# Scores of two heads side by side on 64 rows each, and a new order of work for a pair of heads

## The chip, the cores and the metric

The kernel runs on one core of one Trainium2 chip. The metric is the time on the device of one execution, in microseconds; three runs of the kernel before took 1910.01, 1911.17 and 1916.82 us, and their median is 1911.17 us.

## The reference

A gated cross-attention layer is followed by a gated mixture of experts, all in float32. The input x has 8 batches of 512 tokens of 256 features, the context 8 batches of 1024 keys.

```
q = layernorm(x) @ Wq; k = ctx @ Wk; v = ctx @ Wv        # 8 heads of 64
attn = softmax(q k^T / 8) v, per head
x = x + tanh(g0) * (attn @ Wo + bo)
h = layernorm(x); probs = softmax(h @ router^T)           # 8 experts, the top 2 of each token
pre, gate = rows @ W1[e]^T, rows @ Wg[e]^T                # rows: the tokens of expert e, up to 1280
x = x + tanh(g1) * sum over the two experts of weight * ((pre * silu(gate)) @ W2[e]^T)
```

## The kernel before

Each float32 operand of a product is split into a high part (rounded to the type fp32r, in which TensorE takes one pass) and a low part (the rest); a product is then three matmuls: high by high, high by low and low by high (`passes`, L776 to L781). ScalarE makes the high parts (`hi`), VectorE the low ones (`lo`, L1205).

The attention works batch by batch. A batch is a body of 32 steps; START, FIRST and LAST are written out, six middle batches run in a loop, END finishes the last one. A unit is one head and 128 query tokens (32 units a batch): 128x1024 scores. Unit n = u goes through the engines in steps: TensorE makes its scores in step u (`make_scores`), VectorE their negated maximum (L1491), ScalarE the exponents with the row sum (L1120, a step later), VectorE the reciprocal of the sum (L1501), GpSimd scales the row (L678), TensorE transposes it in eight 128x128 pieces (`turn`, in step u + 2), ScalarE and VectorE split the transposed halves into pt_h and pt_l (in step u + 3). The scores are in four PSUM banks, two units; the transposed unit is in two banks, and `turn` waits until VectorE has read the half that it overwrites (L812).

In the scores the 128 rows of the array hold one head twice: k_st has the 64 rows of a head's high part of k, and in the other 64 rows its low part, q_h has the high part of q twice, and q_l its low part twice. Four matmuls of 512 columns then make one unit (L798 to L804).

The other two PSUM banks are a ring. Everything else that TensorE computes is a job that fills the next bank of the ring: q, k and v projections of the heads to come, o (attention output of one head and 256 tokens, sixteen matmuls), w (its product with Wo for 128 tokens), x and h (transposes of the normalised input of the next batch and of the normalised sum of the batch before), l (router logits) and r (ranks of the tokens in the experts' lists). The table `JOBS` (L70) says in which step a job is done; o jobs stand in the odd steps (L98). ScalarE and VectorE empty the banks of step u - 1 in step u (`drain`, L1043 and L1364): its first job ahead of the other work of the step, its second after the maximum. A job waits until the bank two jobs back is empty (L928). A q result is written to both halves of the rows by four instructions on 64 partitions on each of the two engines, a k result by two.

`between` (L1433) puts the steps of layer normalisation and routing, small VectorE instructions that each wait for the one before, in five gaps of a step. GpSimd also normalises (L655), splits the next batch's context (`split_ctx`), adds the bias (L704, once a batch in step 15) and issues the scatter of the routed rows (L666).

The wait of the score matmuls and the order of TensorE in a step are:

```
until(pe, exp_done, at(b, UNITS, u - 1))      # the unit two before is exponentiated
...
make_scores(body, u); the jobs of step u; turn(body, u - 2)
```

After the last batch the kernel ranks tokens and pads lists, and then runs the experts: 36 chunks of 256 rows, three split matmuls per product, TensorE without a break.

## Time and profile before

| | |
|---|---|
| median of three runs | 1911.17 us |
| the profiled execution, and its span | 1914.74 us, 1913.0 us |
| TensorE busy (L801 scores: 512 + 512 matmuls) | 1749.2 us, 91% of the span |
| VectorE, ScalarE, GpSimd busy | 1396.8, 1124.2, 686.6 us |
| mean granted clock of TensorE | 0.973 of full |

Busy time is the union of the instructions of an engine. The ends of matmuls are modelled and overlap the next ones, so what a matmul occupies is read from the starts of two blocks in the time line, not from its printed length.

### The profile page before, as it was taken

To read this page: it belongs to the slowest core of one execution; us is meant where nothing else is said; L and a number is where in the kernel's file an instruction comes from. 1 tells how busy PE (TensorE), PEld (TensorE's weight loads), DVE (VectorE), ACT (ScalarE), POOL (GpSimd) and SP (SyncE) were. 2 spreads that over 40 slices of the span, in tenths; PEclk is the share of its full clock that TensorE was granted. 3 is DMA by queue.
4 is the path that set the end of the run, shared out by engine and by line. 5 is a ranking of instruction groups with operands and counts; after the bars stand their busy time and mean duration, and the time that the engine had idled before them with its cause. 6 is when DMAs were issued, how large, how long until landed. Compare 5 with 4: busy or idle time off the path is not lost. (4 is left out here: it accounts for less than half of the span.)

```text
span 1913.0 us, 38524 instructions
## 1 busy us (share of the span) xinstructions
PE 1749.2 (91%) x12942; PEld 1629.6 (85%) x12943; DVE 1396.8 (73%) x2955; ACT 1124.2 (59%) x2259; POOL 686.6 (36%) x619
## 2 busy tenths in 40 slices
PE   5899998998998998998998999559999999999998
PEld 4788887987887887887887888459999999999998
DVE  5888888888898888889898888655545645555443
ACT  4767656666766666666776776334545545445443
POOL 3352344344244245244343433423332322333232
PEclk9999999999999999999999999779999999999999
DMA  6100001001011001000000002233133132231211
GB/s 180 34 12 12 23 24 35 23 23 35 12 34 35 12 23 40 18 23 31 16 23 28 18 23 76 91 104 98 30 100 94 28 99 62 61 98 28 33 28 28
DMA packets 65148, 85.88 MB, mean 45 GB/s; under 512 B 7208, under 2 KB 53800, under 8 KB 65008
## 3 DMA queue, kind: packets, MB, share of 16 engines
q1 hardware_dynamic: 47680, 64.08, 10.6%
q0 software_dynamic: 15984, 18.82, 5.6%
q8 instruction: 78, 1.28, 0.3%
q10 hardware_dynamic: 1344, 1.20, 0.2%
q14 instruction: 62, 0.51, 0.1%
HBM read 54.59 MB, written 29.48 MB: 44 GB/s over the span
## 5 line engine op out<-in xcount | busy, mean ns | idle before, releaser
L678 POOL TENSOR_SCALAR probs<-probs,row_rec 128x1024 f32<-128x1024 f32 x256 | 287.7, 1124 | 704.4 <-DVE row_rec L1501 673.9
L1036 ACT ACTIVATE pt_h<-turned 128x512 fp32r<-128x512 f32 x512 | 279.8, 597 | 199.1 <-PE turned L814 194.7
L1207 DVE TENSOR_TENSOR pt_l<-turned,pt_h 128x512 fp32r<-128x512 f32 x512 | 333.6, 684 | 78.4 <-ACT pt_h L1036 76.2
L1491 DVE TENSOR_REDUCE neg_max<-scores 128x1 f32<-128x1024 f32 x256 | 310.9, 1214 | 2.0 <-PE scores L801 1.9
L1120 ACT ACTIVATE probs<-scores,neg_max 128x1024 f32<-128x1024 f32 x256 | 287.2, 1122 | 3.4 <-DVE neg_max L1491 2.4
L814 PE MATMUL turned<-ident,probs 128*128 128x128 f32 x2048 | 272.6, 277 | 10.8 <-POOL probs L678 6.0
L915 PE MATMUL ring<-pt_h,v_hl 128*128 128x256 f32 x1024 | 254.0, 286 | 24.3 <-DVE q_l L1404 9.2
L1658 DVE TENSOR_TENSOR act_f<-ffn,silu 128x256 f32<-128x256 f32 x288 | 122.1, 424 | 193.1 <-ACT silu L1161 180.1
L814 PEld LDWEIGHTS turned<-ident,probs 128*128 128x128 f32 x2048 | 235.3, 143 | 23.5 <-POOL probs L678 10.2
L915 PE MATMUL ring<-pt_l,v_hl 128*128 128x256 f32 x1024 | 251.4, 284 | 0.0
L1161 ACT ACTIVATE silu<-ffn 128x256 f32<-128x256 f32 x288 | 110.4, 383 | 220.3 <-PE ffn L781 212.4
L915 PEld LDWEIGHTS ring<-pt_h,v_hl 128*128 128x128 f32 x1024 | 195.9, 191 | 41.9 <-issue 32.6
L760 POOL DMA_INDIRECT out<-y,y_token x72 | 118.1, 1640 | 247.3 <-DVE y L1629 229.2
L801 PE MATMUL scores<-k_st,q_h 128*128 128x512 f32 x512 | 185.5, 444 | 19.7 <-ACT probs L1120 12.9
L915 PEld LDWEIGHTS ring<-pt_l,v_hl 128*128 128x128 f32 x1024 | 196.5, 192 | 3.7
L1207 DVE TENSOR_TENSOR act_l<-act_f,act_h 128x256 fp32r<-128x256 f32 x288 | 122.2, 424 | 81.4 <-ACT act_h L1036 81.4
L1036 ACT ACTIVATE act_h<-act_f 128x256 fp32r<-128x256 f32 x288 | 120.5, 419 | 96.1 <-DVE act_f L1658 95.8
L779 PE MATMUL ffn<-et_h,w_h 128*128 128x256 f32 x576 | 162.7, 283 | 8.7 <-issue 7.1
L779 PE MATMUL ffn<-w_h,act_h 128*128 128x256 f32 x576 | 165.9, 288 | 0.0
L801 PE MATMUL scores<-k_st,q_l 128*128 128x512 f32 x512 | 162.8, 400 | 0.0
L780 PE MATMUL ffn<-w_l,act_h 128*128 128x256 f32 x576 | 162.5, 282 | 0.0
L780 PE MATMUL ffn<-et_l,wg_h 128*128 128x256 f32 x576 | 161.6, 281 | 0.0
(219 smaller groups left out, 4514.6 us busy)
## 6 DMA issues: line engine op xcount, KB each, us to landing
w_raw<-w_t SPq DMA_DIRECT2D x16, 1024.0 KB, 8.4
e_rows<-lists SPq DMA_DIRECT2D x37, 260.0 KB, 2.7
ctx_raw<-ctx_t SPq DMA_DIRECT2D x16, 512.0 KB, 3.8
wg_raw<-wg_t SPq DMA_DIRECT2D x8, 1024.0 KB, 8.3
lists<-rows SPq DMA_DIRECT2D x8, 520.0 KB, 7.9
x_in<-x SPq DMA_DIRECT2D x8, 512.0 KB, 3.5
x_sum<-x SPq DMA_DIRECT2D x8, 512.0 KB, 3.5
out<-x_sum SPq DMA_DIRECT2D x8, 512.0 KB, 3.0
```

Source lines behind the costliest of these rows:

```text
L678: nc.gpsimd.tensor_scalar(probs[:, k, :], probs[:, k, :], row_rec[:, k:k + 1], 1.0, ALU.mult, ALU.mult).then_inc(scaled, 1)
L760: nc.gpsimd.indirect_dma_start(out[:, :], bass.IndirectOffsetOnAxis(ap=y_token[:, st:st + 1], axis=0), y[:, st, :], None, compute_op=ALU.a ...
L779: nc.tensor.matmul(out_, sh, mh, start=start, stop=False)
L780: nc.tensor.matmul(out_, sh, ml, start=False, stop=False)
L801: last = nc.tensor.matmul(scores[:, u % 2, cols], part[:, buf, ab, q * P:(q + 1) * P], k_st[:, buf, ab, cols], start=part is q_h, stop=par ...
L814: last = nc.tensor.transpose(turned[:, kt, :], probs[:, n % 2, kt * P:(kt + 1) * P], ident[:, :])
L915: last = nc.tensor.matmul(bank[:, 0:2 * P], v_hl[:, kt, h, :], part[:, m, kt, :], start=kt == 0 and part is pt_h, stop=kt == KT - 1 and pa ...
L1036: return nc.scalar.activation(dst, src, ACT.Copy)
L1120: nc.scalar.activation(probs[:, k, :], scores[:, k, :], ACT.Exp, bias=neg_max[:, k:k + 1], accum_out=row_sum[:, k:k + 1])\
L1207: return nc.vector.tensor_tensor(dst, src, hi_part.bitcast(F32), ALU.subtract)
L1491: nc.vector.tensor_reduce(neg_max[:, k:k + 1], scores[:, k, :].rearrange("p (a c) -> p a c", a=2), AX.XY, ALU.max, negate=True).then_inc(n ...
L1658: nc.vector.tensor_tensor(act_f[:, c % 2, :], ffn1[:, c % 4, 0, :], silu[:, :], ALU.mult).then_inc(act_done, 1)
```

## The change

A pair of units is now the same 128 tokens of two heads, A and B. k_h, k_l, q_h and q_l hold the two heads in the upper and the lower 64 rows, and the scores of both are made in even steps by twelve matmuls of 64 rows and 512 columns, head A and head B in turn, each into its own banks. Every engine has a new order in a pair of steps, and `JOBS` is a new table. probs has four buffers instead of two. The o jobs stand in steps 1 and 2 of every four; the first for head A, the second for head B. A o job waits for the units of its own head, and w jobs for the o jobs that they read (those lines are not shown). `high_turned`, `exponent`, `highest` and `low_turned` hold the instructions of L1084 to L1091, L1118 to L1123, L1490 to L1493 and L1425 to L1431 with the new buffer numbers; VectorE empties a q or k bank with one instruction, as ScalarE does. Other moves: Wo's second half is split in step 9 instead of 8, the last weights of the start in 26 instead of 25 on ScalarE, the layer normalisation of the sum in the gaps from step 7 to 11, the routing from step 21 instead of 19; on LAST the loads of the first expert's weights wait for the jobs q 3, k 3 and v 1.

```diff
JOBS = {
-    0: [("k", 1, 0), ("q", 1, 0)], 2: [("k", 1, 1), ("v", 0, 3)], 4: [("w", 1, 0), ("w", 1, 1)],
-    6: [("w", 1, 2), ("w", 1, 3)], 8: [("v", 1, 0), ("q", 2, 0)], 10: [("v", 1, 1), ("k", 2, 0)],
-    12: [("k", 2, 1), ("v", 1, 2)], 14: [("v", 1, 3), ("h", 0, 0)], 15: [("h", 1, 0)],
-    16: [("q", 3, 0)], 17: [("l", 0, 0)], 18: [("k", 3, 0), ("k", 3, 1)],
-    20: [("w", 0, 0), ("w", 0, 1)], 22: [("w", 0, 2), ("w", 0, 3)], 24: [("x", 0, 0), ("x", 1, 0)],
-    25: [("r", 0, 0)], 26: [("q", 0, 0), ("v", 0, 0)], 28: [("v", 0, 1), ("k", 0, 0)],
-    30: [("k", 0, 1), ("v", 0, 2)],
+    0: [("v", 0, 3), ("w", 1, 0)],
+    1: [("w", 1, 1)],
+    2: [("k", 1, 0)],
+    3: [("v", 1, 0)],
+    4: [("k", 1, 1), ("q", 1, 0)],
+    5: [("w", 1, 2)],
+    7: [("w", 1, 3)],
+    8: [("v", 1, 1)],
+    9: [("v", 1, 2)],
+    10: [("k", 2, 0)],
+    11: [("k", 2, 1)],
+    12: [("v", 1, 3), ("q", 2, 0)],
+    14: [("h", 0, 0), ("h", 1, 0)],
+    16: [("w", 0, 0), ("w", 0, 1)],
+    18: [("q", 3, 0)],
+    19: [("l", 0, 0)],
+    20: [("k", 3, 0), ("w", 0, 2)],
+    22: [("k", 3, 1)],
+    23: [("x", 0, 0), ("x", 1, 0)],
+    24: [("w", 0, 3), ("q", 0, 0)],
+    26: [("v", 0, 0)],
+    27: [("r", 0, 0)],
+    28: [("k", 0, 0), ("k", 0, 1)],
+    29: [("v", 0, 1)],
+    31: [("v", 0, 2)],
 }
-NEXT_FROM = 24
-END_STEPS = 27
+NEXT_FROM = 23
+END_STEPS = 29
...
-            if u % 2 == 1 and (prev if u < 5 else own):
-                mine.append(("o", ((u - 5) % UNITS) // 2, 0))
+            if u % 4 in (1, 2) and (prev if u < 5 else own):
+                mine.append(("o", ((u - 5) // 4 * 2 + u % 4 - 1) % (2 * H), 0))
...
-        k_st = tile(attn, "k_st", [P, 2, 2, M], F32R)
-        q_h = tile(attn, "q_h", [P, 2, 2, N], F32R)
-        q_l = tile(attn, "q_l", [P, 2, 2, N], F32R)
+        k_h = tile(attn, "k_h", [P, 2, M], F32R)
+        k_l = tile(attn, "k_l", [P, 2, M], F32R)
+        q_h = tile(attn, "q_h", [P, 2, N], F32R)
+        q_l = tile(attn, "q_l", [P, 2, N], F32R)
...
-        probs = tile(attn, "probs", [P, 2, M])
+        probs = tile(attn, "probs", [P, 4, M])
...
@@ GpSimd, run @@
-                    if body.own if u > 1 else body.prev:
-                        k = u % 2
-                        pool.wait_ge(rec_done, at(b, UNITS, u - 1))
+                    if u % 2 == 0 and (body.own if u > 0 else body.prev):
+                        pool.wait_ge(rec_done, at(b, UNITS // 2, u // 2))
                         alone(pool)
-                        nc.gpsimd.tensor_scalar(probs[:, k, :], probs[:, k, :], row_rec[:, k:k + 1],
-                                                1.0, ALU.mult, ALU.mult).then_inc(scaled, 1)
+                        for n in (u - 2, u - 1):
+                            k = n % 4
+                            nc.gpsimd.tensor_scalar(probs[:, k, :], probs[:, k, :],
+                                                    row_rec[:, k:k + 1], 1.0,
+                                                    ALU.mult, ALU.mult).then_inc(scaled, 1)
-                        if body.own and 27 <= u < 27 + QT:
-                            for k in range(2):
-                                scatter(b - 1, 2 * (u - 27) + k)
+                        if body.own and u in (29, 30):
+                            for k in range(QT):
+                                scatter(b - 1, QT * (u - 29) + k)
-                        if u == 20:
+                        if u == 24:
...
                             split_ctx(b + 1, 0)
-                        if u == 23:
+                        if u == 26:
                             split_ctx(b + 1, 1)
...
@@ TensorE @@
             def make_scores(body, u):
-                b, h, q = body.b, u // QT, u % QT
-                buf, ab = (h // 2) % 2, h % 2
+                b, pair, q = body.b, u // (2 * QT), u // 2 % QT
+                buf, toks = pair % 2, slice(q * P, (q + 1) * P)
...
-                until(pe, exp_done, at(b, UNITS, u - 1))
-                for part in (q_h, q_l):
+                until(pe, exp_done, at(b, UNITS, u))
+                for n, (st, mv) in enumerate(((q_h, k_h), (q_h, k_l), (q_l, k_h))):
                     for half in range(2):
                         cols = slice(half * 512, (half + 1) * 512)
-                        last = nc.tensor.matmul(scores[:, u % 2, cols],
-                                                part[:, buf, ab, q * P:(q + 1) * P],
-                                                k_st[:, buf, ab, cols],
-                                                start=part is q_h, stop=part is q_l)
-                last.then_inc(scores_done, 1)
+                        for ab in range(2):
+                            head = slice(ab * DH, (ab + 1) * DH)
+                            last = nc.tensor.matmul(scores[:, ab, cols], st[head, buf, toks],
+                                                    mv[head, buf, cols], start=n == 0, stop=n == 2)
+                            if n == 2 and half == 1:
+                                last.then_inc(scores_done, 1)
...
             def run(body):
                 for u, jobs in enumerate(body.steps):
-                    if body.own:
+                    if body.own and u % 2 == 0:
                         make_scores(body, u)
+                    if body.prev if u < 2 else body.own:
+                        turn(body, u - 2)
                     for what, c in jobs:
                         reads = wait_for_job(body, u, what)
                         wait_all_drained(pe, body, reads + [c - 2])
                         do_job(what, ring[:, c % 2, :])
-                    if body.prev if u < 2 else body.own:
-                        turn(body, u - 2)
...
@@ ScalarE, drain @@
                 if kind == "q":
-                    for ab in range(2):
-                        for half in range(2):
-                            last = nc.scalar.activation(q_h[half * DH:(half + 1) * DH, i % 2, ab, :],
-                                                        bank[ab * DH:(ab + 1) * DH, :], ACT.Copy,
-                                                        scale=SCALE)
+                    last = nc.scalar.activation(q_h[:, i % 2, :], bank, ACT.Copy, scale=SCALE)
                 if kind == "k":
-                    for ab in range(2):
-                        head = slice(ab * DH, (ab + 1) * DH)
-                        last = hi(k_st[head, i % 2, ab, j * 512:(j + 1) * 512], bank[head, :])
+                    last = hi(k_h[:, i % 2, j * 512:(j + 1) * 512], bank)
...
@@ ScalarE, run @@
+                    first = len(jobs) if u % 2 == 0 else 1
+                    for what, c in jobs[:first]:
                         drain(body, u - 1, what, c)
+                    if body.own and u % 2 == 1:
+                        exponent(b, u)
+                    for what, c in jobs[first:]:
+                        drain(body, u - 1, what, c)
+                    if body.prev if u < 2 else body.own:
+                        high_turned(b, u - 2)
+                    if body.own and u % 2 == 0:
+                        exponent(b, u)
+                    if body.prev and u == 21:
                         wait_drained(act, body, body.where[("l", 0, 0)])
                         nc.scalar.activation(gate[:, 1, :, :], gate[:, 0, :, :], ACT.Exp)\
                             .then_inc(gate_exp, 1)
...
@@ VectorE, run @@
+                    first = len(jobs) if u % 2 == 0 else 1
+                    for what, c in jobs[:first]:
                         drain(body, u - 1, what, c)
                     between(body, u, 0)
+                    if body.own and u % 2 == 0:
+                        highest(b, u)
+                        highest(b, u + 1)
                     between(body, u, 1)
+                    if body.own and u % 2 == 1:
+                        k = (u - 1) % 4
+                        v.wait_ge(exp_done, at(b, UNITS, u + 1))
+                        nc.vector.reciprocal(row_rec[:, k:k + 2], row_sum[:, k:k + 2])\
+                            .then_inc(rec_done, 1)
+                    for what, c in jobs[first:]:
+                        drain(body, u - 1, what, c)
                     between(body, u, 2)
+                    if body.prev if u < 2 else body.own:
+                        low_turned(b, u - 2, 0)
+                        between(body, u, 3)
+                        low_turned(b, u - 2, 1)
```

## Rows read from the trace of the kernel before

**Rows 1.** the page: busy us (share of the span); busy tenths in 40 slices
```profile
PE 1749.2 (91%) x12942; PEld 1629.6 (85%) x12943; DVE 1396.8 (73%) x2955; ACT 1124.2 (59%) x2259; POOL 686.6 (36%) x619
...
PE   5899998998998998998998999559999999999998
...
DVE  5888888888898888889898888655545645555443
```

**Rows 2.** windows: stretch, length, busy PE, PEld, DVE, ACT, POOL (instructions), clock, DMA
```profile
540.00:690.00 150.00, 137.73 (x955) 123.22 (x954) 129.85 (x258) 100.76 (x191) 59.76 (x56) 0.99 0.08 26
...
1350.00:1913.00 563.00, 546.66 (x4641) 544.27 (x4639) 294.46 (x739) 265.85 (x639) 172.08 (x128) 1.00 0.27 58
```

**Rows 3.** line L704: count, duration min/median/max, first and last start
```profile
L704 POOL TENSOR_TENSOR x_sum<-x_sum,bias_o x8: 2405/2422/2449, 98.1 to 1134.7; 128x1024 f32<-128x1024 f32 x8
```

**Rows 4.** time line of TensorE: start, merged length, instruction; 607 to 615 us
```profile
607.27 0.28 PE L915 MATMUL ring<-pt_h,v_hl 128*128 128x256 f32 x1
...
609.18 1.04 PE L814 MATMUL turned<-ident,probs 128*128 128x128 f32 x8
...
609.98 0.72 PE L801 MATMUL scores<-k_st,q_h 128*128 128x512 f32 x2
...
610.99 0.39 PE L779 MATMUL ring<-ctx_h,wk_h 128*128 128x512 f32 x1
...
612.38 0.28 PE L779 MATMUL ring<-wv_h,ctx_h 128*128 128x256 f32 x1
...
613.82 1.04 PE L814 MATMUL turned<-ident,probs 128*128 128x128 f32 x8
```

**Rows 5.** time line, 540 to 640 us: waits of TensorE, and one of VectorE
```profile
550.03 1.92 PE L898 MATMUL ring<-rw,ctx_raw 128*128 128x8 f32 x16 [1.71 <-DVE q_l L1404]
...
620.46 0.73 PE L801 MATMUL scores<-k_st,q_h 128*128 128x512 f32 x2 [1.88 <-ACT probs L1120]
...
620.12 0.42 DVE L1207 TENSOR_TENSOR ot_l<-ring,ot_h 128x256 fp32r<-128x256 f32 x1 [1.80 <-issue]
```

**Rows 6.** instruction groups of VectorE, 246 to 1134 us, shapes apart: busy, mean ns
```profile
L1491 DVE TENSOR_REDUCE neg_max<-scores 128x1 f32<-128x1024 f32 x190 | 230.7, 1214 | 1.5 <-PE scores L801 1.5
...
L1207 DVE TENSOR_TENSOR k_st<-ring,k_st 64x512 fp32r<-64x512 f32 x96 | 66.1, 688 | 16.5 <-ACT k_st L1036 14.9
...
L1404 DVE SCALAR_TENSOR_TENSOR q_l<-ring,q_h 64x512 fp32r<-64x512 f32 x96 | 66.1, 688 | 21.8 <-ACT q_h L1059 20.8
...
L1207 DVE TENSOR_TENSOR pt_l<-turned,pt_h 128x512 fp32r<-128x512 f32 x380 | 247.8, 684 | 60.5 <-ACT pt_h L1036 58.8
...
L1501 DVE RECIPROCAL row_rec<-row_sum 128x1 f32<-128x1 f32 x190 | 29.3, 154 | 0.7
```

**Rows 7.** instruction groups of ScalarE, same stretch
```profile
L1036 ACT ACTIVATE pt_h<-turned 128x512 fp32r<-128x512 f32 x381 | 208.3, 596 | 155.9 <-PE turned L814 152.7
...
L1120 ACT ACTIVATE probs<-scores,neg_max 128x1024 f32<-128x1024 f32 x190 | 213.2, 1122 | 3.1 <-DVE neg_max L1491 2.4
...
L1120 ACT ACTIVATION_READ_ACCUMULATOR probs<-scores,neg_max 128x1 f32 x190 | 40.0, 210 | 0.0
...
L1059 ACT ACTIVATE q_h<-ring 64x512 fp32r<-64x512 f32 x93 | 55.0, 592 | 4.8 <-PE ring L781 3.5
...
L1036 ACT ACTIVATE k_st<-ring 64x512 fp32r<-64x512 f32 x96 | 56.8, 591 | 36.0 <-PE ring L781 35.4
```

**Rows 8.** instruction groups of GpSimd, same stretch
```profile
L678 POOL TENSOR_SCALAR probs<-probs,row_rec 128x1024 f32<-128x1024 f32 x190 | 213.5, 1124 | 518.6 <-DVE row_rec L1501 494.7 <-DVE norm L1251 23.4
...
L666 POOL DMA_INDIRECT lists<-rows,list_row x48 | 48.6, 1012 | 11.4 <-issue 9.5 <-DVE row_rec L1501 1.8
```

**Rows 9.** windows again, the slice behind the boundary; two matmuls in it
```profile
621.00:624.00 3.00, 3.00 (x10) 2.36 (x9) 1.99 (x4) 0.00 (x0) 0.81 (x1) 0.63 0.00 0
...
622.09 0.63 PE L781 MATMUL ring<-ctx_h,wk_l 128*128 128x512 f32 x1
...
622.52 0.63 PE L779 MATMUL ring<-ctx_h,wk_h 128*128 128x512 f32 x1
```

More of the change, by code:

```diff
@@ L82 @@
 CONSTS = 16
-NEXT_FROM = 24
-END_STEPS = 27
+NEXT_FROM = 23
+SLOT_OF = {job: u for u, jobs in JOBS.items() for job in jobs}
+END_STEPS = 29
 class Body:
@@ L124, in place @@
     def place(self, job):
-        if job[0] != "x" and (job[1] > 0 or job == ("v", 0, 3)):
+        if SLOT_OF[job] < NEXT_FROM:
             return self.where[job]
@@ L832, in wait_for_job @@
                         pe.wait_ge(weights_split, 5)
-                    reads = [body.where[("o", H * i + H - 2 + j // 2, 0)]]
+                    o = ("o", H * i + H // 2 + 1 + j // 2 * 2, 0)
+                    reads = [body.before.where[o] - RING if i == 1 and j < 2 else body.where[o]]
                 if kind == "x":
@@ L1070, in drain @@
                 if kind == "o":
-                    toks = slice((i % 2) * 2 * P, (i % 2 + 1) * 2 * P)
-                    last = hi(ot_h[:, (i // 2) % 4, toks], bank[:, 0:2 * P])
+                    h, m = i // 4 * 2 + i % 2, i // 2 % 2
+                    last = hi(ot_h[:, h % 4, m * 2 * P:(m + 1) * 2 * P], bank[:, 0:2 * P])
                 if kind == "x":
@@ L1075, in drain, with high_turned, exponent @@
                 last.then_inc(hi_done[kind], 1)
+            def high_turned(b, n):
+                toks = slice((n // 2 % 2) * P, (n // 2 % 2 + 1) * P)
+                for j in range(2):
+                    act.wait_ge(turned_done, at(b, 2 * UNITS, 2 * n + j + 1))
+                    keys = slice(4 * j, 4 * j + 4)
+                    hi(pt_h[:, n % 2, keys, toks], turned[:, keys, :]).then_inc(pt_hi, 1)
+            def exponent(b, n):
+                k = n % 4
+                act.wait_ge(neg_done, at(b, UNITS, n + 1))
+                nc.scalar.activation(probs[:, k, :], scores[:, n % 2, :], ACT.Exp,
+                                     bias=neg_max[:, k:k + 1], accum_out=row_sum[:, k:k + 1])\
+                    .then_inc(exp_done, 1)
             def run(body):
@@ L1080, in run @@
                     jobs = body.results(u)
-                    for what, c in jobs[:1]:
+                    first = len(jobs) if u % 2 == 0 else 1
+                    for what, c in jobs[:first]:
                         drain(body, u - 1, what, c)
-                    if body.prev if u < 3 else body.own:
-                        n = u - 3
-                        toks = slice((n % 2) * P, (n % 2 + 1) * P)
-                        for j in range(2):
-                            act.wait_ge(turned_done, at(b, 2 * UNITS, 2 * n + j + 1))
-                            keys = slice(4 * j, 4 * j + 4)
-                            hi(pt_h[:, (n // 2) % 2, keys, toks], turned[:, keys, :])\
-                                .then_inc(pt_hi, 1)
-                    if body.prev and u == 19:
+                    if body.own and u % 2 == 1:
[7 more added lines that the diff above has]
+                    if body.prev and u == 21:
                         wait_drained(act, body, body.where[("l", 0, 0)])
@@ L1096, in run @@
                             .then_inc(gate_exp, 1)
-                    for what, c in jobs[1:]:
-                        drain(body, u - 1, what, c)
                     if body is END and u == 8:
@@ L1400, in drain @@
                 if kind == "q":
[L1401 to L1412 removed]
+                    last = nc.vector.scalar_tensor_tensor(
+                        q_l[:, i % 2, :], bank, SCALE, q_h[:, i % 2, :].bitcast(F32),
+                        ALU.mult, ALU.subtract)
+                if kind == "k":
+                    keys = slice(j * 512, (j + 1) * 512)
+                    last = lo(k_l[:, i % 2, keys], bank, k_h[:, i % 2, keys])
                 if kind == "v":
```

101 lines of the change are left out of this document (37 added, 64 removed).

## The prediction

> **What bounds the kernel now.** I read the page first. TensorE is busy 91% of the span, VectorE 73%; in the slices VectorE stands at 8 and 9 only in the first two thirds, the attention, and falls to 5 behind it [rows 1]. So the two parts have to be taken apart, by windows. The expert part, 563 us from 1350 us on, has TensorE busy 546.7 us [rows 2], and between the parts lie some slices with TensorE at 5 [rows 1]; the change doesn't touch either. What it touches is the attention: the bias addition runs once a batch, first at 98.1 and last at 1134.7 us [rows 3], so a batch takes 148.1 us on average; the middle ones are near 150. In 150 us about one middle batch long TensorE is busy 137.7 us and VectorE 129.9 [rows 2]. TensorE sets the time there, VectorE is close behind. The other 12.3 us are TensorE's waits; by the releasers they are mostly a VectorE that is late in emptying a ring bank, 1.71 us at the router's job for a q result, and 1.88 us at the batch boundary [rows 5].
>
> **TensorE's work, from the time line** [rows 4]. The starts of successive blocks give what each really occupies: eight transposes 0.80 us (609.18 to 609.98), the four score matmuls of a unit 1.01 us (609.98 to 610.99), a k job of six 512-column matmuls 1.39 us, so 0.232 each, a v job of twelve 256-column ones 1.44, an output job of sixteen 1.91 (607.27 to 609.18), 0.119 each. The 0.39 us printed for one matmul is its depth, not its share.
>
> **Part 1, the scores.** Removed for two units: eight matmuls with 128 rows, 2.02 us. Added: twelve with 64 rows and 512 columns. No row shows a matmul with 64 rows. Bounds: run one behind the other, 12 x 0.232 + 0.08 (what a block costs above its matmuls now: 1.01 - 4 x 0.232) = 2.86 us; if the two heads' matmuls run at once, 6 x 0.232 + 0.08 = 1.47 us. The latter asks for one weight load and one matmul each 0.116 us, which the output job already does at 0.119 [rows 4]; the two heads write different banks, read different partitions and need different rows of the array, so nothing that a row shows is shared, and I take the lower value as the base. Against it stands that the array must change its shape before and after the block. What this costs lies between nothing and the depth left in the pipe, 0.39 - 0.23 = 0.16 us a time [rows 4], twice a pair; I take half, 0.17 in all. So 1.64 us against 2.02: 0.38 a pair, times 16 pairs, times 8 batches: **49 us less** (ends: 70 less, and 108 more).
> The Trainium skill has a rule for each side. "TensorE: Matmul & The Clock Gate", Part 3 (packing small matmuls), says that matmuls on distinct row groups start within some 4 ns of each other; no run here shows it yet, and by it alone the block would be 1.47 us. "TensorEngine Tiling (Array Packing)", Key Properties, says that a change of tiling mode drains TensorE; by it both changes are paid in full, 1.79 us, and this part is worth 29 us. That rule is the second rival below.
>
> **Part 2, emptying the ring.** A q result took VectorE four instructions of 0.688 us and is now one; a k result took two and is now one [rows 6]. Per batch 4 x 3 x 0.688 + 8 x 0.688 = 13.8 us less of VectorE. The same edits on ScalarE, at 0.59: 11.8 us less [rows 7]. I price the wider instruction as the narrow one, since a 128x512 pass of pt_l also took 0.684. None of it is on the path itself: VectorE goes from 129.9 to 116 us a batch. What it gives is that late banks come sooner, which is counted in part 4. The reciprocals keep 0.154 each for two columns, 16 fewer, 2.5 us.
>
> **Part 3, the new round of a pair.** Let S be the moment at which the scores of both heads are there. VectorE then runs both maxima, to S + 2.5, and only then the low part of the first turned head: first half done at S + 3.3, second at S + 3.95 [rows 6]. ScalarE splits that head until S + 1.8, exponentiates A to S + 3.1, empties a first bank, and finishes exponent B at S + 5.1 [rows 7]. The next scores wait for B. TensorE: transposes of A, 0.8; jobs of the even step J0; transposes of B, the second half of which waits for S + 4.0; jobs of the odd step J1. So the transposes of B wait about 2.7 - J0. From the new table J0 is 2.8 us or more in 13 of 16 pairs; it is one output job (1.91) at u = 6 and 30 and one v job (1.44) at u = 8: waits 0.8 + 0.8 + 1.3 = 2.9 us a batch. The next scores find exponent B done (S + 1.6 + J0 + J1 against S + 5.1) except at u = 15, which has no job: 0.65. The jobs of odd steps wait for the first bank of the even step, which VectorE empties only behind the low part: 0.2 in six pairs, 1.2. The second x transposes at u = 23 wait for the second bank, emptied behind exponent B (5.1 + 0.6 + 0.7 against 5.5): 0.9. At u = 21 VectorE waits for the router's exponent, which ScalarE now does behind the high part of B; reciprocals, then maxima are late by 1.6, of which slack hides half: 0.7. Queued behind this wait are the reciprocals and the low part of B; GpSimd waits for them. GpSimd's two scalings, 1.12 each [rows 8], start at S + 5.3 and end at S + 6.4 and 7.6; the transposes need them from the next S, at the earliest S + 6.7, and S + 10. Hidden, by 0.3 us in the shortest pair; if this cover goes, it costs 0.3 to 1 us in such a pair. Its scatters (1.01 each), now four at a time, fall at the head of the pairs 28 and 30, 4 us in a queue that is free for 5 [rows 8].
>
> **Part 4, the sum of waits.** The boundary wait of 1.88 us stays: VectorE has 1.80 us of its own issue there too, and both stand at the loop's back edge [rows 5]. Behind it the granted clock reads 0.63 for the slice, between the two levels of 2.4 and 1.2 GHz, and a 512-column matmul takes 0.43 us (622.09 to 622.52) instead of 0.23 [rows 4, 9]. That stays as well. New total: 1.9 + 2.9 + 0.65 + 1.2 + 0.9 + 0.7 = 8.2, and I take 9 for what I overlooked, against 12.3: 3.2 a batch, **25 us less**. Ends: all new waits hidden, 6 left, 50 less; as many waits as now, 0.
> What moves in the first and last stretch (two more steps at the end, h together, l two steps later, ctx split later) is issued beside DMA waits or in steps without scores: 0, ends -3 and +3.
>
> **The sum.** 49 + 25 = 74 us. The profiled execution took 1914.7 us around its span of 1913.0; less 74, 1840.7. The median shown is 3.6 below that execution, so I forecast **1837 us**. (Within 0.5%, 1902 to 1921 us, is what I call the same.)
>
> **Rivals.** *A, the two heads don't run side by side* (the one that ends slower). For it: no row has two matmuls on the array at once. Against: the issue rate and separate banks. Place: every score block. Price: + 0.84 us a pair, 108 us, less the 25 of waits: 1911 + 83 = 1994 us. It decides as soon as a matmul of 64 rows occupies more than 0.168 us of the stream, since 12 of these are the 2.02 of now.
> *B, the change of shape is paid in full.* Block 1.79 us, 29 us instead of 49: 1857. For it: the printed depth; against: today's blocks of transposes and scores follow with 0.08 between them.
> *C, the round binds.* The maxima of both heads stand ahead of the low part, and both exponents must be done before the next scores: today's order has two units in flight and needs neither. If each pair loses 0.4 us beyond my list, 0.4 x 16 x 8 = 51: 1888, and with B 1908. For it: S + 4 and S + 5.1 leave margins of 0.1 to 0.7 in most pairs. Against: both engines lose 12 to 16 us a batch.
> *D, the clock.* Should two further waits a batch be as long as the boundary's, each would cost its 1.9 and again about 1.6 at the lower level: 2 x 3.5 x 8 = 56, 1893.
> *E, everything fits*: 70 + 50: 1911 - 120 = 1791.
>
> **Chances.** Forecast, with its waits between 6 and 11 and half a drain give or take: 0.50; B 0.16; E 0.05; C 0.12; D 0.05; A 0.12. Of C and D 0.05 ends within 0.5% of now and 0.01 beyond it; with A 0.12 slower; faster 0.83. Range: from 1797, just above E, to 1888, at C. The forecast's own range is 1810 to 1865.
>
> **What would show it.** Right: a score block of 1.5 to 1.8 us for two units, the second head's matmul starting with the first's; a batch of about 140 us; VectorE near 116 us busy in it, ScalarE near 89; waits before the transposes at u = 7, 9 and 31; the same 1.9 us at the boundary. Wrong in part 1: score matmuls spaced by 0.23. Wrong in part 3: waits before the scores on exponents in most pairs, or before the transposes on scaled. The expert part should keep its 563 us.

## The result and the profile after

The changed kernel takes **1841.05 us** (median of 4 runs, 1839.40 to 1841.53) against 1913.99 us (1910.01 to 1916.82) for the kernel before, run beside it: ratio 0.962, 95% interval 0.960 to 0.964. The forecast was 1837 us, 1797 to 1888. In the sessions of the experiments the kernel before had medians of 1911.8 to 1913.6 us, so their times are set directly against 1841 us; differences of 1 or 2 us are noise.

The page of the changed kernel, as [rows 1]:

```profile
PE 1714.6 (93%) x13454; PEld 1567.4 (85%) x13455; DVE 1264.9 (69%) x2667; ACT 1020.8 (55%) x2099; POOL 682.8 (37%) x619
...
PE   4899999999999999999999997299999999999997
...
DVE  4687887887887887887888886554654646546443
```

VectorE lost 132 us of work over the run, 16.5 a batch, and its digits in the attention fell from 8 and 9 to 7 and 8; TensorE's are 9 from the third slice to the end of the attention. The bias addition once a batch, as [rows 3], and the windows of a batch length, of the slice behind a batch boundary and of the expert part, as [rows 2, 9]:

```profile
L727 POOL TENSOR_TENSOR x_sum<-x_sum,bias_o x8: 2392/2427/2434, 98.6 to 1059.3; 128x1024 f32<-128x1024 f32 x8
```

```profile
510.00:647.00 137.00, 132.09 (x1001) 114.68 (x998) 110.52 (x214) 87.27 (x168) 57.00 (x54) 0.99 0.09 29
584.00:587.00 3.00, 2.58 (x13) 1.62 (x13) 0.69 (x1) 0.60 (x1) 0.96 (x1) 0.63 0.05 11
1277.00:1839.00 562.00, 546.40 (x4638) 543.89 (x4636) 294.08 (x739) 265.75 (x638) 171.76 (x128) 1.00 0.27 58
```

The first bias addition ends the start, the last ends the batches. Start 98.1 -> 98.6 us; seven batches 1036.6 -> 960.7, so a batch 148.1 -> **137.2**; the rest 778.3 -> 780.5. The 73 us of span all come from the batches. The experts keep their time, as forecast (TensorE busy 546.4 of 562). In a batch VectorE is busy 110.5 us and ScalarE 87.3, where 116 and 89 were forecast.

Two causes can be told apart by one window of 800 us inside the attention, laid over both kernels (before, then after):

```profile
240.00:1040.00 800.00, 736.01 (x5046) 659.42 (x5044) 691.40 (x1371) 533.43 (x1003) 318.88 (x294) 0.98 0.08 26
```

```profile
240.00:1040.00 800.00, 771.47 (x5852) 670.04 (x5851) 645.29 (x1268) 504.62 (x975) 338.85 (x315) 0.99 0.09 28
```

TensorE idles 8.0% of 148.1 us, 11.8 a batch, before, and 3.6% of 137.2, 4.9, after; its busy time goes from 136.3 to 132.3. So of 10.9 us a batch **6.9 are waits and 4.0 are TensorE's own time**. The forecast had 3.2 and 6.1. (Part of the 4.0 is the granted clock's; see *The clock* below.)

The time line of TensorE over one pair, as [rows 4]:

```profile
522.91 0.28 PE L942 MATMUL ring<-pt_l,v_hl 128*128 128x256 f32 x1
523.12 0.74 PE L828 MATMUL scores<-k_h,q_h 64*128 64x512 f32 x4
523.69 0.63 PE L828 MATMUL scores<-k_l,q_h 64*128 64x512 f32 x4
524.16 0.62 PE L828 MATMUL scores<-k_h,q_l 64*128 64x512 f32 x4
524.71 1.09 PE L840 MATMUL turned<-ident,probs 128*128 128x128 f32 x8
525.57 0.36 PE L942 MATMUL ring<-pt_h,v_hl 128*128 128x256 f32 x1
```

The block is 523.12 to 524.71, 1.59 us. Its twelve matmuls start in pairs, one of each head: 558 such pairs start between 236 and 1050 us, half of them within 4 ns, as the forecast asked for. Ahead of it 0.21 us pass instead of 0.12, and the eight transposes behind it occupy 0.86 instead of 0.79 or 0.80. With these a pair costs 1.75 us where it cost 2.02 [rows 4]: 0.27 less.

TensorE's waits from 236 to 1020 us, 5.7 batches (total us, times, longest):

```profile
PE scores L828 <- issue: 9.9, 5, 2.2
PE turned L840 <- DVE pt_l L1234: 8.1, 17, 0.7
PE ring L919 <- DVE ot_l L1234: 3.0, 5, 0.6
PE turned L840 <- issue: 2.1, 3, 1.1
PE ring L942 <- DVE v_hl L1234: 1.3, 5, 0.3
PE ring L914 <- DVE k_l L1234: 1.2, 6, 0.2
```

The 9.9 us are five passages of the loop's back edge, 1.8 to 2.2 each; the boundary wait that was to stay has stayed. The transposes wait where VectorE's low parts are late, as forecast, but 1.4 us a batch instead of 2.9. No wait on an exponent is there.

### The profile page after: what moved, and what is told of

The parts are those of the page before. It is cut to its first block and busy times, and to the rows that moved or that the text cites. A ratio compares the mean times of both kernels' runs of the same rounds, so it can differ in the third digit from the quotient of the medians.

```text
span 1839.8 us, 38882 instructions
## 1 busy us (share of the span) xinstructions
PE 1714.6 (93%) x13454; PEld 1567.4 (85%) x13455; DVE 1264.9 (69%) x2667; ACT 1020.8 (55%) x2099; POOL 682.8 (37%) x619
## 3 DMA queue, kind: packets, MB, share of 16 engines
q1 hardware_dynamic: 47680, 64.08, 10.9%
## 5 line engine op out<-in xcount | busy, mean ns | idle before, releaser
L1450 DVE TENSOR_REDUCE neg_max<-scores 128x1 f32<-128x1024 f32 x256 | 301.5, 1219 | 56.0 <-PE scores L828 55.3
L840 PEld LDWEIGHTS turned<-ident,probs 128*128 128x128 f32 x2048 | 226.1, 142 | 96.9 <-issue 53.8
L840 PE MATMUL turned<-ident,probs 128*128 128x128 f32 x2048 | 284.2, 280 | 23.9 <-DVE pt_l L1234 16.9
L942 PE MATMUL ring<-pt_h,v_hl 128*128 128x256 f32 x1024 | 263.6, 295 | 5.9 <-DVE k_l L1234 4.1
L805 PE MATMUL ffn<-et_h,w_l 128*128 128x256 f32 x576 | 161.4, 280 | 0.0
L805 PE MATMUL ffn<-w_h,act_l 128*128 128x256 f32 x576 | 161.3, 280 | 0.0
```

The costliest lines, as they stand in the source:

```text
L805: return nc.tensor.matmul(out_, sl, mh, start=False, stop=stop)
L840: last = nc.tensor.transpose(turned[:, kt, :], probs[:, n % 4, kt * P:(kt + 1) * P], ident[:, :])
L942: last = nc.tensor.matmul(bank[:, 0:2 * P], v_hl[:, kt, h, :], part[:, ab, kt, :], start=kt == 0 and part is pt_h, stop=kt == KT - 1 and p ...
L1450: nc.vector.tensor_reduce(neg_max[:, k:k + 1], scores[:, n % 2, :].rearrange("p (a c) -> p a c", a=2), AX.XY, ALU.max, negate=True).then_i ...
```

## The experiments

A kernel's batch length below is the distance of its first and last bias addition over seven.

**1. The two heads one after the other.**

```diff
-for n, (st, mv) in enumerate(((q_h, k_h), (q_h, k_l), (q_l, k_h))):
-    for half in range(2):
-        for ab in range(2):
+for ab in range(2):
+    for n, (st, mv) in enumerate(((q_h, k_h), (q_h, k_l), (q_l, k_h))):
+        for half in range(2):
```

> The changed kernel with the twelve 64-row score matmuls in another order: all six of head A, then all six of head B, so that no two neighbours are on different rows. Same instructions, same number. Theory (neighbours on different rows run at once; the block took 1.60 us): now nothing overlaps but the last of A with the first of B, the block is 12 x 0.232 + 0.2 = about 2.8 us (2.99 less one overlapped slot), 1.2 us a pair more, x 128 = 150 us: about 1990 us, perhaps 10 to 30 less because waits shrink under a longer TensorE. Rival (64-row matmuls are simply cheap, each 0.12 to 0.13 us of the stream whatever stands beside it): 1841 us, no change.

Measured 1893.98 us, ratio 0.990 (0.987 to 0.992): 53 us more than the change, neither number. One block in TensorE's time line:

```profile
545.19 0.73 PE L828 MATMUL scores<-k_h,q_h 64*128 64x512 f32 x2
545.76 0.39 PE L828 MATMUL scores<-k_l,q_h 64*128 64x512 f32 x1
545.77 0.49 PE L828 MATMUL scores<-k_h,q_h 64*128 64x512 f32 x1
546.00 0.39 PE L828 MATMUL scores<-k_l,q_h 64*128 64x512 f32 x1
546.11 0.39 PE L828 MATMUL scores<-k_h,q_h 64*128 64x512 f32 x1
...
546.46 0.39 PE L828 MATMUL scores<-k_h,q_l 64*128 64x512 f32 x1
...
547.36 1.10 PE L839 MATMUL turned<-ident,probs 128*128 128x128 f32 x8
```

The program issues all six of head A, then six of head B. The records show B's first (k_h,q_h at 545.77) start with A's third (k_l,q_h at 545.76), ahead of A's remaining three, and from there the two heads take turns, 0.11 to 0.12 us apart. The block is 2.17 us: not 1.59, and not the 12 x 0.232 = 2.78 of a strict line. So TensorE does run 64-row matmuls of the two halves at once, and by the recorded starts it reaches past queued ones to do so; the full gain comes only when the two heads alternate. Rival A is out. The Trainium skill, "TensorE: Matmul & The Clock Gate", Part 3, says that matmuls start in program order without exception; these records disagree.

**2. The new order with scores of 128 rows.** The same steps and buffers, eight 128-row matmuls a pair. The kernel sums the scores of both heads and leaves k_l out, so it doesn't compute the reference; it prices the work only.

```diff
-for n, (st, mv) in enumerate(((q_h, k_h), (q_h, k_l), (q_l, k_h))):
+for st in (q_h, q_l):
...
-            last = nc.tensor.matmul(scores[:, ab, cols], st[head, buf, toks], mv[head, buf, cols], ...)
+            last = nc.tensor.matmul(scores[:, ab, cols], st[:, buf, toks], k_h[:, buf, cols], ...)
```

> The changed kernel, with each pair's scores made by eight 128-row matmuls of 512 columns instead of twelve of 64 rows (both heads' rows are summed and k_l is left out, so these are not the scores of the reference; all other work is unchanged). It prices the side-by-side scores alone inside the new order. Theory: block 8 x 0.232 + 0.08 = 1.94 to 2.02 us and no change of shape, against 1.60 and about 0.1 ahead of it: 0.3 to 0.35 us a pair, 38 to 45 us: 1880 to 1886 us. Rival (the new order is all of the gain): 1841 to 1850. Rival (side by side is all of it): 1905 or more.

Measured 1852.90 us, 0.969 (0.967 to 0.970): only **12 us** more than the change, just above the rival of 1841 to 1850 and far from the theory. The block:

```profile
545.63 1.09 PE L827 MATMUL scores<-k_h,q_h 128*128 128x512 f32 x4
546.55 1.08 PE L827 MATMUL scores<-k_h,q_l 128*128 128x512 f32 x4
547.47 1.03 PE L840 MATMUL turned<-ident,probs 128*128 128x128 f32 x8
548.26 0.36 PE L942 MATMUL ring<-pt_h,v_hl 128*128 128x256 f32 x1
```

Eight matmuls in one block take 1.84 us (545.63 to 547.47), not the 2.02 of two blocks of four. The lead-in of 0.08 is paid once, and some more. Of the 0.27 us that a pair gained, 0.18 thus comes from putting the two units into one block and only 0.09 from the rows: 0.25 in the block, less 0.09 ahead of it and 0.07 behind it. In the two profiles 4.5 of the 12 us lie ahead of the first bias addition (103.1 us against 98.6; granted clock of the first 100 us 0.93 against 0.97) and 6.1 in the seven batches.

**3 and 4. The narrow emptying put back**, in the changed kernel (3) and in that of experiment 2 (4). The latter is the new order, with its merged score block, and nothing else of the change; like experiment 2 it doesn't compute the reference.

```diff
-last = nc.scalar.activation(q_h[:, i % 2, :], bank, ACT.Copy, scale=SCALE)
+for ab in range(2):
+    head = slice(ab * DH, (ab + 1) * DH)
+    for dst in (q_l, q_h):
+        last = nc.scalar.activation(dst[head, i % 2, :], bank[head, :], ACT.Copy, scale=SCALE)
```

(On VectorE alike: four for a q bank, two for a k bank on both engines.)

> The changed kernel, with the q and k banks emptied again by four and two instructions of 64 partitions x 512 on each of ScalarE and VectorE (the second copies of q go where nobody reads them). VectorE gets 13.8 us a batch back, ScalarE 11.8. Theory (the emptying is hidden, but late banks make TensorE wait): TensorE's waits grow by 1 to 3 us a batch, 8 to 24 us in all: 1849 to 1865. Rival (it is off the path altogether): 1841 to 1844. Rival (it carries all of the 7 us a batch by which the waits fell): 1890 or more.

> Both of the above together: what is left of the change is the new order of work and the new table of projections (the scores again sum two heads and leave k_l out). If the parts add, 1841 + 40 + 15 = about 1896 us, so the new order alone is worth some 18 us of the 73. If the order is worth nothing without the other two, 1914. If it is worth most, below 1880.

Measured 1982.80 us, 1.037 (1.035 to 1.039), and 1987.93, 1.039 (1.037 to 1.041). For experiment 3 only the rival of 1890 or more holds, and it too expected far less than the 142 us found; for 4 all three expectations fell. The same work that cost VectorE 13.8 and ScalarE 11.8 us a batch in its instructions [rows 6, 7] costs the kernel 17.4 us a batch here: a batch is 154.7 us. How, shows in the time lines of experiment 3 (ScalarE, VectorE, TensorE):

```profile
565.52 0.58 ACT L1087 ACTIVATE q_l<-ring 64x512 fp32r<-64x512 f32 x1
565.99 0.59 ACT L1087 ACTIVATE q_h<-ring 64x512 fp32r<-64x512 f32 x1
...
567.09 0.58 ACT L1087 ACTIVATE q_h<-ring 64x512 fp32r<-64x512 f32 x1
567.70 1.09 ACT L1063 ACTIVATE pt_h<-turned 128x512 fp32r<-128x512 f32 x2
```

```profile
567.71 0.68 DVE L1437 SCALAR_TENSOR_TENSOR q_l<-ring,q_h 64x512 fp32r<-64x512 f32 x1 [0.47 <-ACT q_h L1087]
...
569.82 0.71 DVE L1437 SCALAR_TENSOR_TENSOR ring<-ring,q_h 64x512 f32<-64x512 f32 x1
570.56 1.29 DVE L1240 TENSOR_TENSOR pt_l<-turned,pt_h 128x512 fp32r<-128x512 f32 x2
```

```profile
571.30 0.92 PE L840 MATMUL turned<-ident,probs 128*128 128x128 f32 x5 [0.92 <-DVE pt_l L1240]
```

ScalarE's four q copies hold the high part of the turned scores until 567.70; VectorE waits for the last copy, then its own four hold the low part to 570.56; the next transposes, whose banks these are, start 0.92 us late at 571.30. The two bursts add, one behind the other, and these transposes are next in TensorE's order. Waits of TensorE are 19.7 us a batch (12.7% of 154.7), against 4.9.

**5 and 6. The price of the change of shape, alone.** One extra matmul of eight columns ahead of each first output job, 128 in all, once with 64 rows and once with 128.

```diff
+nc.tensor.matmul(bank[:, 0:8], v_hl[0:64, 0, h, :], pt_h[0:64, ab, 0, 0:8], start=True, stop=True)
```

> The changed kernel with one more matmul ahead of each o job's first: 8 columns, 64 rows, into the bank that the job overwrites. 128 of them in the attention. It stands between matmuls of 128 rows, so the array changes shape twice for it. Theory (a change of shape costs about 0.09 us on the way in and up to 0.28 on the way out and behind): 128 x 0.2 to 0.35 = 26 to 45 us above its twin with 128 rows. Rival (what the score block loses beside 6 x 0.232 is something of its own, such as the first weights of two heads): within 5 us of the twin.

> The twin: the same small matmul with 128 rows, no change of shape. Either theory: 128 x (0.03 to 0.07 us) = 4 to 9 us above the changed kernel, 1845 to 1850.

Measured 1900.72 us, 0.994 (0.993 to 0.996), and 1871.73, 0.979 (0.977 to 0.980). The difference, 29 us over 128, is **0.23 us for a change of shape and back**, as the expectation had it (0.2 to 0.35); the forecast took 0.17, its rival B 0.32. The time line of experiment 2 against that of the change gives 0.16 for the part that shows at the edges of the score block. The Trainium skill, "TensorEngine Tiling (Array Packing)", Key Properties, says that the change of mode drains the engine; the runs agree in so far as the change has a price.

That the 128-row twin itself cost 31 us was a miss. Part of it is in its waits:

```profile
308.07 0.50 PE L828 MATMUL scores<-k_h,q_h 64*128 64x512 f32 x2 [2.17 <-issue]
311.05 0.80 PE L828 MATMUL scores<-k_h,q_h 64*128 64x512 f32 x2 [2.49 <-issue]
```

```profile
PE scores L828 <- issue: 23.4, 10, 2.6
```

Sixteen more matmuls in the loop's body, and the passage of the back edge stalls twice, 2.17 and 2.49 us, with two matmuls between: 13.5 us more of this wait than in the change. The profile names no engine that it waits for there.

**7. The old order with wide emptying.** The kernel before with one instruction for each q and k bank, its scores the same four matmuls of 128 rows a unit. In the kernel before each head stands in both halves of the rows, which is why its banks were emptied in halves; with wide emptying these scores sum two heads and leave k's low part out. So this kernel, too, prices the work only and is no replacement: it is the layout of the change, one head in each half, that lets a kernel which computes the reference empty a bank with one instruction.

```diff
-for ab in range(2):
-    for half in range(2):
-        last = nc.scalar.activation(q_h[half * DH:(half + 1) * DH, i % 2, ab, :], bank[ab * DH:(ab + 1) * DH, :], ...)
+last = nc.scalar.activation(q_h[:, i % 2, 0, :], bank, ACT.Copy, scale=SCALE)
```

> The kernel before, with q and k banks emptied by one instruction of 128 partitions on each engine, as in the changed kernel, and scores from four 128-row matmuls a unit that read these (two heads summed, low part of k left out). Old order, old table. VectorE loses 13.8 us a batch, ScalarE 11.8. In the new order the same step was worth 135 us (1988 to 1853). Theory (the new round has a closed loop of VectorE and ScalarE that narrow banks stretch; the old order keeps two units in flight and hides more of it): the old order gains 6 to 9 us a batch, its waits for q_l and x_sum, 50 to 70 us: 1845 to 1865, so the new order itself is worth 0 to 12 us. Rival (the new order is needed to gain from wide banks): 1890 or more.

Measured 1828.69 us, 0.956 (0.954 to 0.958): **less time than the whole change**, and below its expectation. Its window and its bias additions:

```profile
240.00:1040.00 800.00, 765.08 (x5441) 698.53 (x5440) 657.66 (x1349) 508.86 (x965) 338.97 (x310) 1.00 0.08 27
```

```profile
L704 POOL TENSOR_TENSOR x_sum<-x_sum,bias_o x8: 2410/2418/2431, 87.0 to 1053.1; 128x1024 f32<-128x1024 f32 x8
```

A batch is 138.0 us, as in experiment 2 (138.1), so the new order gives nothing in a batch, although its merged score block takes 16 x 0.18 = 2.9 us less; what takes these back was not followed. But the first bias addition is at 87.0 against 98.6 in the change and 103.1 in experiment 2: the new order loses its time at the start. The kernel of this experiment with an unrolled loop or an earlier start wasn't run. And here TensorE's busy share fell as well, with the same matmuls: 92.0% of 148.1 us is 136.3, 95.6% of 138.0 is 132.0. The granted clock is 1.00 in this window and was 0.98 before. The clock rose as the waits went; by the estimate under *The clock* it explains 2.8 of these 4.3 us a batch. No term of the forecast had this.

**8. The low half between the maxima** of A and B on VectorE, against the transposes' waits.

```diff
 highest(b, u)
+if turns:
+    low_turned(b, u - 2, 0)
 highest(b, u + 1)
```

> The changed kernel, with VectorE's even step in the order maximum A, first low half of the turned head, maximum B. Theory (TensorE's transposes of B wait for the low halves, 2.2 us a batch): the first half is read 1.2 us sooner, exponent B is behind exponent A on ScalarE anyway: 1 to 2 us a batch less, 1825 to 1835. Rival (exponent B and so the next scores are on the loop too, by 0.7 us a pair): 1841 or slower, up to 1860.

Measured 1849.42 us, 0.967 (0.965 to 0.968): 8 us slower, as the rival had it, and the wait that it was to shorten grew from 8.1 to 15.9 us:

```profile
PE turned L840 <- DVE pt_l L1234: 15.9, 23, 1.2
```

The second maximum, and with it the exponent and the low parts of B, come later; that this costs more than the first half brings is argued, not tested.

**9. The start.** The splits of the first wk and wv two jobs earlier on ScalarE and one on VectorE, and Wo's split on VectorE one step later.

```diff
-if body is START and u in (19, 26):    # ScalarE
+if body is START and u in (19, 24):
...
-if body is START and u in (19, 26):    # VectorE
+if body is START and u in (19, 25):
...
-if body is FIRST and u in (5, 9):      # VectorE
-    half = (u - 5) // 4
+if body is FIRST and u in (6, 10):
+    half = (u - 6) // 4
```

> The changed kernel with its start regrouped and nothing else: ScalarE and VectorE split the first wk and wv one and two jobs of the score stage earlier, and the split of Wo on VectorE moves from the head of the next stage to its quarter points. In the changed kernel the value projections start at 24.86 us of the span and the first scores at 33.96, where the old order with wide emptying has 19.46 and 28.18; and VectorE waits 3.23 us at 55.56 for the Wo split, TensorE 4.12 at 57.54. Theory (the start was mis-priced at 0): 5.4 us from the first and 3 to 5 from the second, 1831 to 1833. Rival (something else sets the start, such as the landing of the inputs or the queue): within 3 us of 1841.

Measured 1829.49 us, 0.956 (0.954 to 0.957): 11.6 less. The wait of TensorE in the start of the changed kernel, which is gone, and the first scores of the new one:

```profile
24.86 0.55 PE L803 MATMUL ring<-wv_h,ctx_h 128*128 128x256 f32 x1 [5.09 <-issue]
```

```profile
28.41 0.73 PE L828 MATMUL scores<-k_h,q_h 64*128 64x512 f32 x4
```

The first scores come at 28.41 instead of 33.96, the first bias addition at 84.7 instead of 98.6, with the batches as long as before. The listed 8.4 to 10.4 us are exceeded by 1 to 3; what these are wasn't followed. Which of the two moves brings how much was not tested apart.

**10. No loop.** The six middle batches written out.

```diff
-with eng.Fori(1, B - 1) as b:
+for b in range(1, B - 1):
```

> The changed kernel with its six middle batches written out instead of looped, so that the engines pass no back edge. Each of the five back edges shows about 2 us (1.76 to 2.21) of wait on TensorE ahead of the first scores, and the quartets right behind it run at 0.72 to 0.85 us instead of 0.58 to 0.60. Theory (the back edge itself costs this): 5 x (2.0 + 0.7 to 1.5), so 12 to 18 us less, 1823 to 1829. Rival (the wait at the edge of a batch is on the exponents and the queue and comes back as a named wait, or fetching the longer code costs as much): 1838 or more.

Measured 1826.62 us, 0.955 (0.953 to 0.956): 14.4 less, within the theory. The two largest of TensorE's waits from 236 to 1020 us, and the window (the other two waits are 1.3 and 1.2 us, as before):

```profile
PE turned L840 <- DVE pt_l L1234: 12.1, 29, 0.8
PE ring L919 <- DVE ot_l L1234: 3.4, 5, 0.7
```

```profile
240.00:1040.00 800.00, 780.66 (x5981) 680.43 (x5981) 658.66 (x1294) 516.02 (x997) 347.81 (x325) 1.00 0.09 28
```

The wait on issue is gone; with the 2.1 ahead of the transposes it was 12.0 us, and a third of that comes back as waits on VectorE's low parts (8.1 to 12.1 us). A batch is 134.7 us, the granted clock 1.00. In the changed kernel the clock behind the back edge is 0.63 over 3 us (the window of 584 above) and the score quartets take 0.72 and 0.85 us instead of 0.57 and 0.47; this is so behind the edges at 304, 443 and 584 us, while behind those at 723 and 861 the clock stays 1.00. The Trainium skill, "Runtime: NRT & Kernel Launch", Instruction fetch mechanics, says that a branch to a place that isn't held makes the engine wait until its code is fetched; the traces agree, with about 2 us each, and with 85 packets in each of the two instruction queues of the changed kernel against 70 and 40 without the loop. The kernel of experiment 6 has the same 85, so its second stall is not explained by their count.

**11. The router's exponent ahead of the exponent of B** in step 21.

```diff
+if body.prev and u == 21:
+    wait_drained(act, body, body.where[("l", 0, 0)])
+    nc.scalar.activation(gate[:, 1, :, :], gate[:, 0, :, :], ACT.Exp).then_inc(gate_exp, 1)
 if body.own and u % 2 == 1:
```

(and taken away from its place behind the exponent)

> The changed kernel with the router's exponent on ScalarE moved ahead of the second head's exponents in job 21, nothing else. VectorE waits 8.2 us in all over six times (1.4 us a batch) for that exponent. Theory (VectorE has slack of some 20 us a batch, so its waits cost little): 0 to 3 us less, 1838 to 1841. Rival (what VectorE does behind the wait is on TensorE's path): 8 less, 1833; and the other way, exponent B later by 0.4 us holds up the transposes at 22 and 23: 3 us more, 1844.

Measured 1842.65 us (1840.62 to 1847.16), 0.964 (0.962 to 0.965): no change. VectorE's wait for this exponent, 8.2 us in the change, is no longer listed, and no gain is seen: the 0.7 us a batch that the forecast gave this step were covered.

**12. The earlier start and no loop together**, the edits of 9 and 10.

> The changed kernel with both the earlier start and the batches written out, the router's exponent where it was. The two act on different stretches (the first 100 us, and the edges of the batches), measured at 11.6 and 14.4 us less than the changed kernel. Theory (they add): 1841 - 26 = 1815, between 1812 and 1818, ahead of the old order with wide emptying (1829). Rival (the head start is taken by the first batch of the unlooped code, so they overlap): 1822 to 1828.

Measured **1811.59 us**, 0.948 (0.946 to 0.949), the fastest, and it computes the reference. The two add, and a little more (11.6 + 14.4 = 26.0 expected, 29.5 found, just below the range of 1812 to 1818). The bias addition:

```profile
L727 POOL TENSOR_TENSOR x_sum<-x_sum,bias_o x8: 2391/2434/2442, 84.6 to 1027.7; 128x1024 f32<-128x1024 f32 x8
```

The start is that of 9 (84.6), the batches are 134.7 us as in 10.

## Why the prediction came out right, and where it was wrong

The total is 4 us from the measured one, and that is luck: three terms erred and cancel. The forecast added 49 (scores), 25 (waits) and 0 (ends). Measured per batch and times eight, TensorE's own time gave 32 us and the waits 55; eight batches at 10.9 us would be 87 us, but 73 came, so the ends took 14 back.

| edit | us | from |
|---|---|---|
| new order alone, on the kernel before | +74 | 1988 - 1914 |
| wide emptying, in the new order | -135 | 1853 - 1988 |
| 64 rows side by side | -12 | 1841 - 1853 |
| wide emptying, in the old order | -85 | 1829 - 1914 |

The kernels of 1988, 1853 and 1829 us don't compute the reference (experiments 4, 2, 7). The new order includes the merged score block.

*Part 1, the scores: mechanism right, size off.* Two things were off. The base of 2.02 was that of two blocks with work between, and the change also merges them: as one block the same matmuls take 1.84. And the change of shape shows mostly outside of the block: 1.59 us in it, 1.75 with its edges, against 1.64 forecast and 1.79 by rival B, which was nearer here and whose total of 1857 failed on the other terms. A pair gains 0.27, not 0.38, which is 35 us over 128 pairs instead of 49, and only 12 of these are the rows'. Rival A is out.

*Part 2, emptying: the failed step.* "None of it is on the path itself" was wrong. The row that spoke against it was there: a 1.71 us wait of TensorE on a q result's low part [rows 5], and idle time of VectorE ahead of it for ScalarE's q_h, 20.8 us [rows 6]. A burst of two or four emptying instructions on ScalarE, and then again on VectorE, stands ahead of the splitting of a turned head, and TensorE's transposes wait for that. Priced alone, its removal is 10.1 us a batch in the old order and 16.5 in the new, for 13.8 us of VectorE's instructions. Of the 10.1, TensorE's waits are 5.8 (from 11.8 to 6.0, 4.4% of 138.0) and its busy time 4.3. In the old order it is by itself more than the gain of the whole change.

*Part 3, the new round.* The waits that it listed came to 6.35 us a batch beside the boundary's; measured are about 2.8 (8.1 + 3.0 + 2.1 + 1.3 + 1.2 over 5.7 batches). Of the transposes named (u = 7, 9, 31) that at u = 9 waits, 0.59 us in the batch from 443 us on; u = 25 and 29, which weren't named, wait 0.66 and 0.21. No wait on an exponent is seen in the middle batches. Yet this round is worth nothing by itself: alone it makes the kernel 74 us slower, as rival C would have it in kind, and it is saved by the wide emptying that it came with. The list was made for the round with the wide emptying in it, so it could not show this.

*Part 4, the waits.* 11.8 fell to 4.9 a batch, 6.9 less instead of 3.2: 55 us over eight batches, not 25. The boundary's stayed, as forecast, at 1.8 to 2.2 us, with a lower clock behind it three times in five. It was read as a wait to be kept; experiment 10 shows that it is the loop's, and that it goes.

*The ends: "0, ends -3 and +3".* The first bias addition came 0.5 us later, and this hid a loss. Wide emptying alone brings the first bias addition to 87.0 (old order); the changed kernel has it at 98.6. The late split of the first weights and of Wo costs 11.6 us, as experiment 9 shows; the forecast wrote that it lay beside DMA waits, and TensorE waited 5.09 us there.

*The clock.* The forecast saw it fall behind the boundary only [rows 9]. In the kernel before it fell behind four of the six router jobs from 249 to 1001 us too, each of which waits 1.70 us for q_l; this is the wait that rows 5 show at 550 us, and there, as at 1001, the clock did not fall:

```profile
249.17 3.05 PE L898 MATMUL ring<-rw,ctx_raw 128*128 128x8 f32 x16 [1.70 <-DVE q_l L1404]
```

```profile
250.00:257.00 7.00, 7.00 (x28) 6.33 (x28) 4.49 (x8) 2.29 (x4) 1.11 (x1) 0.53 0.27 75
...
551.00:558.00 7.00, 6.29 (x39) 5.19 (x39) 5.88 (x12) 3.36 (x6) 2.25 (x2) 1.00 0.24 77
```

(A row of the time line, and two windows behind such jobs.) Wide emptying takes this wait away, and with it the falls: none is left in experiment 7, behind back edges of 1.5 to 2.2 us included, and none at a router job of the changed kernel. Summed over windows of 2 us from 240 to 1040, the lost clock is an estimated 15 us before, 7 in the changed kernel and 0 in experiment 7: 2.8, 1.2 and 0 a batch. So some 1.6 of the 4.0 us of "TensorE's own time" in the change are the clock's, and the q_l wait cost more than its length. Rival D had the mechanism with the opposite sign.

*Slips in its sums.* Half of 0.32 is 0.16, not 0.17; 12.3 less 9 is 3.3, not 3.2; VectorE's 116 us leaves out the 2.5 us of reciprocals that part 2 counts; the chance of a slower kernel adds up to 0.13, not 0.12. None moves the total by more than 2 us.

Open: the batch of experiment 1 is 6.1 us longer than the change's, where 16 x 0.58 us of block less 1.5 us of waits make 7.8; and of the 31 us of the 128-row twin in experiment 6 the added stalls explain 13.5, and 128 issues of 0.11 us (445.33 to 445.44 in its time line) another 14; with some 7 for the clock, which falls behind all five of its back edges instead of three, that is 3 to 4 more than found. And the 0.27 us of a pair (4.3 a batch) and the 1.6 of the clock are 1.9 more than the 4.0 measured.

## What to carry to other kernels

Where two engines empty a bank one after the other, halving the instructions of both can be worth more than their share of busy time says; price a burst by what stands behind it on both engines, not by the slack of the busier one. Before crediting a packed matmul, write the same matmuls as one block: most of the gain may be the merged block, and the change of shape is paid at its edges. Look at the granted clock behind every repeated wait, not behind one of them. A new order is measured alone and at its ends too, since a loss in the start disappears behind a gain in the batches.

## What the runs showed of the hardware

- Emptying 64 or 128 partitions of 512 columns takes nearly the same: 0.688 and 0.689 us on VectorE, 0.591 and 0.600 on ScalarE [rows 6, 7]. Groups of the changed kernel, 236 to 1059 us:

```profile
L1234 DVE TENSOR_TENSOR k_l<-ring,k_h 128x512 fp32r<-128x512 f32 x48 | 33.1, 689 | 8.2 <-ACT k_h L1063 7.8 <-issue 0.3
```

```profile
L1063 ACT ACTIVATE k_h<-ring 128x512 fp32r<-128x512 f32 x48 | 28.8, 600 | 4.1 <-PE ring L805 4.1
```

- A change from 128 rows to 64 and back costs 0.23 us (29 us over 128).
- 64-row matmuls on the two halves of the rows run at once: starts 4 ns apart (median of 558 pairs), the block of twelve 1.59 us. Those of the free half start ahead of queued ones of the busy half (545.77 before 546.00 in experiment 1).
- A back edge of the changed kernel costs TensorE 1.8 to 2.2 us, and twice that in a body longer by 16 matmuls (2.17 and 2.49); writing the loop out gave 14.4 us for the five, what came back as other waits and went with the clock included.
- The granted clock can fall behind a repeated wait of 1.7 us, and not each time: 0.53 at 250 us, 1.00 at 551 us in the kernel before.
